# A windowed attention on one NeuronCore: key-side scores recomputed, or query-side weights transposed

## What is computed

```python
q = heads(x @ Wq + bq); k = heads(x @ Wk + bk); v = heads(x @ Wv + bv)
# key index runs over s-128 .. s+128, clipped to the sequence
scores = einsum('bhsd,bhswd->bhsw', q, k_win) / sqrt(8)
scores = where(valid, scores, -inf)
attn = softmax(scores, axis=-1)
out = einsum('bhsw,bhswd->bhsd', attn, v_win)
return out.transpose(0, 2, 1, 3).reshape(B, S, E) @ Wo + bo
```

## Time and profile before

| | us |
|---|---|
| median of 3 runs | 3092.83 (3081.48 to 3099.36) |
| the profiled execution: its time | 3103.04 |
| its span in the trace | 3101.3 |
| PE, DVE, ACT, POOL busy | 2707.9, 1738.0, 1476.6, 1833.4 |
| mean granted PE clock over the span | 0.873 |

### The profile page before, as it was taken

One profiled execution on the slowest core, in us unless ns is written; L12 is line 12 of the kernel. 1 busy time (PEld: TensorE's weight loads), 2 busy tenths in 40 slices (PEclk: granted clock), 3 DMA queues, 4 the chain that ended last, 5 costly groups with the idle time before them and its releaser, 6 DMA issues. The chain is left out here.

```text
span 3101.3 us, 91235 instructions
## 1 busy us (share of the span) xinstructions
PE 2707.9 (87%) x37375; PEld 1824.3 (59%) x37375; DVE 1738.0 (56%) x3395; ACT 1476.6 (48%) x2703; POOL 1833.4 (59%) x3112
## 2 busy tenths in 40 slices
PE   4859999965989999989999999999999958999977
PEld 1228888852666666666666666666666635455445
DVE  5832222214767776677767777777777635334324
ACT  3722232212656666566666566656665622233233
POOL 0045666405988888888888887888888711121111
PEclk9967898756999999999999999999999987577668
DMA  1001111102111212122212212121111100000000
GB/s 31 0 22 34 44 38 35 30 17 110 52 42 50 60 52 71 50 57 60 59 48 63 67 52 57 52 78 43 42 49 45 43 11 13 1 1 1 1 12 14
DMA packets 113143, 124.58 MB, mean 40 GB/s; under 512 B 40782, under 2 KB 71262, under 8 KB 111966
## 3 DMA queue, kind: packets, MB, share of 16 engines
q1 hardware_dynamic: 111808, 117.52, 13.8%
q10 hardware_dynamic: 926, 1.27, 0.1%
HBM read 35.89 MB, written 8.91 MB: 14 GB/s over the span
## 5 line engine op out<-in xcount | busy, mean ns | idle before, releaser
L1719 POOL TENSOR_TENSOR l_rot_a<-l_rot_a,l_rot_b 128x512 f32<-128x512 f32 x384 | 483.9, 1275 | 109.8 <-DVE l_rot_b L1579 109.3
L1207 PE MATMUL l_A<-l_wts,l_H 128*128 128x512 f32 x768 | 416.1, 626 | 25.5 <-ACT l_H L1520 21.5
L1573 DVE TENSOR_TENSOR l_rot_a<-l_A,l_tab 128x512 f32<-128x512 f32 x384 | 264.9, 690 | 288.5 <-ACT l_sq L1439 276.2
L1728 POOL TENSOR_TENSOR l_qk<-l_rot_a,l_rn 128x512 f32<-128x512 f32 x384 | 388.7, 1044 | 21.2 <-POOLq L1766 20.9
L1439 ACT ACTIVATE l_sq<-l_A 128x512 f32<-128x512 f32 x384 | 231.0, 601 | 131.9 <-PE l_A L1207 128.3
L1445 ACT ACTIVATE l_pT<-l_T 128x512 f32<-128x512 f32 x192 | 108.8, 595 | 374.0 <-PE l_T L1253 373.7
L1579 DVE TENSOR_TENSOR l_rot_b<-l_A,l_tab 128x512 f32<-128x512 f32 x384 | 261.4, 681 | 0.0
L1583 DVE TENSOR_REDUCE l_ss<-l_sq 128x8 f32<-128x512 f32 x384 | 259.5, 676 | 0.0
L2048 ACT ACTIVATE a_pT<-a_t 128x384 f32<-128x384 f32 (+1 forms) x256 | 111.1, 463 | 261.4 <-PE a_t L1946 261.3
L1308 PE MATMUL l_T<-ident,l_qk 128*128 128x128 f32 x1536 | 210.3, 279 | 19.6 <-POOL l_qk L1728 14.4
L1308 PEld LDWEIGHTS l_T<-ident,l_qk 128*128 128x128 f32 x1536 | 174.9, 142 | 84.1 <-issue 58.0
(11 more groups left out here) (340 smaller groups left out, 5948.0 us busy)
## 6 DMA issues: line engine op xcount, KB each, us to landing
l_vw<-l_vn SPq DMA_DIRECT2D x384, 128.0 KB
l_vw<-l_vn SPq DMA_DIRECT2D x360, 64.0 KB
l_wts<-in_l_wts SPq DMA_DIRECT2D x18, 650.0 KB, 4.9
c_lower_out<-c_amt SPq DMA_DIRECT2D x16, 384.0 KB, 2.5
c_inv<-c_first_in SPq DMA_DIRECT2D x16, 384.0 KB, 3.4
l_tab<-in_l_tables SPq DMA_DIRECT2D x6, 1024.0 KB, 5.1
l_wts<-in_l_wts SPq DMA_DIRECT2D x6, 635.5 KB, 5.3
result<-x SPq DMA_DIRECT2D x4, 256.0 KB, 2.3
```

Of the source, the lines that this page charges most:

```text
L1207: pe.matmul(A[j % 2][:], cols(m), w_of(m)[:, C_QKV + 512 * j:C_QKV + 512 * j + 512], start=True, stop=True).then_inc(pq_done, 1)
L1573: dve.tensor_tensor(rot_a[p][:, j, :].rearrange("p (a d) -> p a d", d=DH), src.rearrange("p (a d) -> p a d", d=DH), table[:, a, t:t + 1, : ...
L1719: pool.tensor_tensor(rot_a[m % 2][:, j, :], rot_a[m % 2][:, j, :], rot_b[:, j, :], ALU.add).then_inc(rot_rdy, 1)
L1728: pool.tensor_tensor(qk[:, j, :].rearrange("p (a d) -> p a d", d=DH), rot_a[p][:, j, :].rearrange("p (a d) -> p a d", d=DH), rn[p][:, 8 * ...
```

## The change

`turned`, `turn_maxima` and `shift` go. The scores are made once, with queries on partitions. ACT reads them from `s_ps` with `negmax` as the bias of the exponential and writes `p` (two tiles of 16 x 384). POOL clears the corners of `p`. PE then transposes the weights: a chunk is one group of heads and one neighbouring tile, four transposes of 128x128 into one bank of `t_ps`, 12 chunks a tile (8 at the ends of a sequence), 176 in all. Of every three chunks ACT copies two to `pT` and DVE one. A bank of `s_ps` is now free when the exponential has read it. Values of tile t are made in step t+1, a group at a time, and the output parts come in step t+2. The core of the diff:

```diff
-        negmax = [sb(f"a_negmax{i}", [P, QUADS, P]) for i in range(2)]
-        pT = [sb(f"a_pT{i}", [P, AH, SPAN]) for i in range(RING)]
+        negmax = [sb(f"a_negmax{i}", [P, AH]) for i in range(2)]
+        p = [sb(f"a_p{i}", [P, AH, SPAN]) for i in range(2)]
+        pT = sb("a_pT", [P, 3, AH, P])
...
-        TURNED, VALUED = 2, 4
-        STEPS = NT + VALUED
+        STEPS = NT + 2
...
+        def chunks(t):
+            lo, hi = near(t)
+            return [(j, a) for j in range(QUADS) for a in range(lo, hi + 1)]
+        def by_vector(c):
+            return c % 3 == 2
...
 # tensor engine, scores(t, h)
-                    pe.wait_ge(mx_rdy, n - GROUP + 1)
+                    pe.wait_ge(p_rdy, n - GROUP + 1)
...
+            def turn_weights(t, i):
+                j, a = chunks(t)[i]
+                c = FIRST_CHUNK[t] + i
+                pe.wait_ge(sel_rdy, QUADS * t + j + 1)
+                if c >= 2:
+                    if by_vector(c - 2):
+                        pe.wait_ge(pt_dve, vector_chunks(c - 1))
+                    else:
+                        pe.wait_ge(pt_act, act_chunks(c - 1))
+                for g in range(GROUP):
+                    mm = pe.transpose(t_ps[c % 2][:, P * g:P * g + P], p[t % 2][:, GROUP * j + g, P * (1 + a):P * (2 + a)], ident[:])
+                mm.then_inc(pt_done, 1)
...
             for s in range(STEPS):
-                if has(s):
-                    for h in range(GROUP):
-                        scores(s, h)
-                if has(s - 1):
-                    turn_maxima(s - 1)
-                if has(s - VALUED):
-                    values(s - VALUED, (0, 1))
-                for h in range(GROUP, AH):
+                for h in range(AH):
                     if has(s):
                         scores(s, h)
-                    if has(s - TURNED):
-                        turned(s - TURNED, h - GROUP)
-                    if h == 7 and has(s - VALUED):
-                        values(s - VALUED, (2, 3))
-                    if h == 11 and has(s - VALUED):
-                        turn_out(s - VALUED)
...
+                    if has(s - 1) and h < len(chunks(s - 1)):
+                        turn_weights(s - 1, h)
+                    if h == 1 and has(s - 2):
+                        turn_out(s - 2)
+                    if h == 4 and has(s - 2):
+                        turn_heads(s - 2)
+                    if h == 7 and has(s - 2):
+                        project_out(s - 2)
+                    if h >= AH - QUADS and has(s - 1):
+                        values(s - 1, h - (AH - QUADS))
...
 # scalar engine
-                act.wait_ge(t_done, AH * t + h + 1)
-                act.activation(pT[t % RING][:, h, c0:c1], t_ps[h % 2][:, c0:c1], ACT.Exp).then_inc(p_rdy, 1)
+                act.wait_ge(mx_rdy, n + 1)
+                act.activation(p[t % 2][:, h, c0:c1], s_ps[h % GROUP][:, c0:c1], ACT.Exp, bias=negmax[t % 2][:, h:h + 1]).then_inc(p_rdy, 1)
+            def keep_turned(t, i):
+                act.activation(pT[:, 1 + a, GROUP * j:GROUP * j + GROUP, :].rearrange("k h q -> k (h q)"), t_ps[c % 2][:],
+                               ACT.Copy).then_inc(pt_act, 1)
...
             for s in range(STEPS):
+                if has(s - 2):
+                    keep_out(s - 2)
                 for h in range(AH):
-                    if has(s - TURNED):
-                        weights(s - TURNED, h)
+                    if has(s):
+                        weights(s, h)
+                    if has(s - 1) and h < len(chunks(s - 1)) and not by_vector(FIRST_CHUNK[s - 1] + h):
+                        keep_turned(s - 1, h)
+                    if h == 5 and has(s - 2):
+                        keep_heads(s - 2)
...
 # vector engine
-            def shift(t):
-                dve.tensor_tensor(q, m_ps[:].rearrange("p (j q) -> p j q", j=QUADS), q, ALU.add).then_inc(qa_rdy, 1)
+            def keep_turned(t, i):
+                dve.tensor_copy(pT[:, 1 + a, GROUP * j:GROUP * j + GROUP, :].rearrange("k h q -> k (h q)"), t_ps[c % 2][:])\
+                   .then_inc(pt_dve, 1)
```

More of the change, by code:

```diff
@@ L1919, in around, with act_chunks, vector_chunks @@
             return slice(P * (t + lo), P * (t + hi + 1))
+        def chunks(t):
+            lo, hi = near(t)
+            return [(j, a) for j in range(QUADS) for a in range(lo, hi + 1)]
+        FIRST_CHUNK = [sum(len(chunks(i)) for i in range(t)) for t in range(NT + 1)]
+        def by_vector(c):
+            return c % 3 == 2
+        def act_chunks(c):
+            return c - c // 3
+        def vector_chunks(c):
+            return c // 3
         @block.sync
@@ L1958, in values @@
+            def values(t, j):
                 lo, hi = near(t)
-                if quads[0] == 0:
-                    pe.wait_ge(sel_rdy, QUADS * (t + hi) + QUADS)
+                last_chunk = FIRST_CHUNK[t] + (j + 1) * (hi - lo + 1)
+                pe.wait_ge(pt_act, act_chunks(last_chunk))
+                pe.wait_ge(pt_dve, vector_chunks(last_chunk))
+                if j == 0:
                     pe.wait_ge(x_rdy, t)
[L1962 to L1969, removed]
+                for a in range(lo, hi + 1):
+                    for g in range(GROUP):
+                        h = GROUP * j + g
+                        mm = pe.matmul(o_ps[VW * g:VW * g + VW, P * j:P * j + P], v[:, t + a, VS * h:VS * h + VW],
+                                       pT[:, 1 + a, h, :], start=(a == lo), stop=(a == hi), skip_group_check=True)
@@ L2005, in _ @@
             pe.wait_ge(v_rdy, NC)
[L2006 removed]
+            pe.wait_ge(init, 1)
             for s in range(STEPS):
[L2009 to L2016 removed]
+                for h in range(AH):
                     if has(s):
                         scores(s, h)
[L2019 to L2031 removed]
+                    if has(s - 1) and h < len(chunks(s - 1)):
[8 more added lines that the diff above has]
+                        values(s - 1, h - (AH - QUADS))
         @block.scalar
@@ L2117, in _ @@
             dve.wait_ge(bo_rdy, 1)
[L2118 to L2126, removed]
+            for s in range(STEPS):
+                for h in range(AH):
                     if has(s):
                         maxima(s, h)
-                    if h == 11 and has(s - VALUED):
-                        divide(s - VALUED)
+                    if has(s - 1) and h < len(chunks(s - 1)) and by_vector(FIRST_CHUNK[s - 1] + h):
+                        keep_turned(s - 1, h)
+                    if h == 3 and has(s - 2):
+                        divide(s - 2)
+                    if h == 8 and has(s - 2):
+                        add(s - 2)
             dve.wait_ge(x_rdy, NT)
@@ L2143, in clear @@
                 if lo == -1:
-                    part = pT[t % RING][:, heads, 0:P]
+                    part = p[t % 2][:, heads, 0:P]
                     last = pool.affine_select(out=part, in_=part, pattern=[[0, GROUP], [1, P]], compare_op=ALU.is_ge, fill=0.0,
@@ L2147, in clear @@
                 if hi == 1:
-                    part = pT[t % RING][:, heads, 2 * P:3 * P]
+                    part = p[t % 2][:, heads, 2 * P:3 * P]
                     last = pool.affine_select(out=part, in_=part, pattern=[[0, GROUP], [-1, P]], compare_op=ALU.is_ge, fill=0.0,
```

52 lines of the change are left out of this document (21 added, 31 removed).

## The result

| | before | after |
|---|---|---|
| median, us (4 runs each) | 3096.1 (3081.5 to 3102.1) | 3324.86 (3307.7 to 3332.4) |
| loop of the attention in the profile, us | 414.1 | 645.0 |
| mean granted clock in it | 0.67 | 0.51 |
| PE busy in it, us | 378.1 | 637.8 |

The changed kernel takes 1.0739 times the time of before, 95% interval 1.0682 to 1.0796: 228.8 us more by the medians, where 235 were forecast. The time of 3324.86 is 3 us from the 3328 of the prediction.

What follows compares the result with a forecast made beforehand. PE was taken as the bound: scores, chunks, values and outputs at the lower clock sum to 668.6 us, adjusted to a 649 us loop, 235 over 414.1, giving 3338, or 3328 on the median's level; range 3180 to 3370.

Steps and rivals of the forecast that it cites:

- The bound: Attention loop: PE bounds it, busy 378.1 of 414.1 us before the change; PE busy over 95% expected after.
- added waits: PE's chunk waiting for the copy of the chunk two before, longer-held `s_ps` banks, values waiting for copies: costed at zero.
- lone score: One score standing alone between two changes of shape on PE: 1.58 us at 384 columns, lower clock; the least certain step.
- values of a group: Value matmuls of one head group of a tile on PE, six groups of four: 1.43 us at the lower clock.
- a chunk with `turn_out`: A chunk followed by `turn_out` in the same shape on PE: 1.9 us, the longest full-height run left.
- the 41 us that I kept open downwards: 256 scores on PE: some 0.16 us less each if no weight load lay between their two passes.
- no run over 1.9 us is left: PE's new order: full-height runs too short to lift the clock, so it stays at 0.50 until the last tile.
- second rival: Attention loop: clock goes to 1.00 and stays from step 1's first chunks; loop 358 us, kernel 3037; chance 0.10.
- two sums, 649 and 358: Forecast attention loop in us: 649 wholly at the lower clock, 358 at the upper, against 414 before.
- Do transposes count for the clock?: PE's clock: the normalisation's 16 transposes seemed to lift it; the skill says transpose-mode work doesn't engage the full level.
- third rival: PE starts transposes in the array's free quarters, so lone scores cost less; result near no change; chance 0.05.
- ACT and DVE: Per tile ACT 13.5 us and DVE 12.6, covered by PE's 22 or more; exponential's bias up to 0.1 each, taken as nothing.

Runs made afterwards that it cites:

- groups: The changed kernel's instructions reordered on PE: four scores, then that group's chunks, all values of a tile at the step's end; 2964.5 us, 0.9587 times before.
- pairs: The changed kernel with scores and chunks in twos on PE: two scores, then two chunks; 2989.8 us, 0.9671 times before.
- Lifting the clock: The changed kernel with 32 needless transposes added at the head of steps 2 and 10; two executions, 3204.55 and 3067.54 us.
- its repetition: The changed kernel with 32 needless transposes at the head of steps 2 and 10, measured again; six executions: 3086, 3111, 3134, 3188, 3191, 3201 us.

## Why the prediction was right

- **The bound.** Right. PE is busy for 99% of the loop, and the added waits cost it 0.3 us before a chunk and 4.4 before a score (2.2 of them at 384 columns).
- **The prices at the lower clock.** Forecast and measured: a lone score 1.58 and 1.58 (2800.24 to 2801.82), a chunk 1.04 and 1.04 (2801.82 to 2802.86), the values of a group 1.43 and 1.43 (2828.66 to 2830.09), a chunk with `turn_out` 1.90 and 1.90 (2798.34 to 2800.24). So the 41 us that I kept open downwards, for a lone score cheaper than that, were not needed; no run parts its weight load from its passes. The loop came out at 645.0 against 649. The forecast had priced all of it at the lower level, and in the 3.2 us from 2931.8 and in the last 9 us it was at the upper; the 2.4 us that PE was busy in the first of these would be 4.8 at the lower, so I estimate that the two make up most of the 4 us.
- **The clock.** The level was right: 0.51 in the loop's mean, and 0.829 to 0.836 over the span in all four executions, so it is no chance of one. The reason given for it is only half right, and that part was luck. I had written that in the kernel before the clock rose only after 3.76 us of full-height work. The same trace has rises after less. Two more stretches of the kernel before:

```profile
2703.50:2706.40 2.90, 2.27 (x13) 0.86 (x8) 2.06 (x7) 1.30 (x3) 0.00 (x0) 1.00 0.00 0
2812.80:2815.60 2.80, 2.80 (x17) 1.36 (x20) 1.37 (x6) 0.00 (x0) 0.57 (x1) 0.50 0.00 0
2815.90:2829.00 13.10, 11.75 (x150) 7.49 (x139) 8.04 (x31) 4.80 (x14) 1.27 (x2) 1.00 0.01 2
```

```profile
2814.43 1.11 PE L1954 MATMUL a_m<-ident,a_negmax 128*128 128x128 f32 x4
2815.48 1.64 PE L1967 MATMUL a_o<-a_pT,a_v 128*32 128x128 f32 x48
```

  At 2703 it rose behind 2.72 of values alone, between 2815.6 and 2815.9 within 1.5 us of the end of the scores, and near 2867 even among scores and turned scores. So "no run over 1.9 us is left" was no sound ground for "it will not rise", and the changed kernel did rise at 2931. What the runs do show is the direction: with longer runs of full-height work the clock rose and stayed (groups), mostly stayed (pairs), or rose while added transposes ran, and the order decides over the level with the same instructions. The rule behind it stays open, and holding the level is partly chance, as the executions with two additions show. My second rival (the clock goes up and stays) was a real state of this order, its pair priced rightly (1.43 against 1.42); in the traces it held only with added work. By the prediction's two sums, 649 and 358, the clock is the larger part of what the grouped order gains back (645 to 286): about 290 us by this estimate, and some 70 the grouping.
- **Do transposes count for the clock?** I said so from the earlier trace rows, against the Trainium skill ("TensorE: Matmul & The Clock Gate", Part 4: PE-mode transpose). The grouped order, in which transposes are a large share of PE's work, ran at 1.00 from 2640 on, and under "Lifting the clock" and in its repetition the clock rose each of four times while the 32 transposes of the identity ran. The measurements decide, and they differ from the page. That transposes count as much as values is not shown: in the pairs, 2.75 of transposes twice lifted nothing and 2.62 of values twice did.
- **The third rival** (no emptying between shapes) is out: at the lower level 179 lone scores of 384 columns hold PE for 1.57 or 1.58 each.
- **ACT and DVE.** Right to cost at nothing; the exponential's bias took 0.09 of the up to 0.1 that I allowed. It can matter only once the order is mended: 16 x 0.09 = 1.4 us of ACT in a step of the grouped kernel, an estimate that no run tests.
- **The median.** The move of 235 stood on the loop of one execution of before; between the two loops in the traces it was 231, and by medians 229. That the median came within 3 us of 3328 is closer than this working can claim, with 30 us of spread ahead of the loop.

## What to carry to other kernels

Count array time by shape, not by columns: on PE four 32-row matmuls next to each other cost what one costs alone between two changes of shape, so interleaving kinds of matmul instruction by instruction undoes the sharing. When such a loop runs at the lower clock, try the order first, with the same instructions grouped by shape and full-height work in long runs: here it turned 7% slower into 4% faster, without one matmul more. And when a change halves a kind of work but splits it finely, work out the loop at both clock levels before believing either.

## What was not expected of the hardware

- One kernel, the changed order with two additions, ran at either level of the clock within one execution (156 us at the upper, 297 at the lower), and its eight executions lie between 3068 and 3205 us. At each level it keeps an exact pace, 1.42 or 2.62 us a pair.
- Work that nothing needs made the kernel 206 us faster (3324.86 to 3118.7).
- A per-partition bias from SBUF costs an exponential of 384 columns 0.09 us (0.491 to 0.580). The Trainium skill ("ScalarE: Activation LUTs", What ACT_TABLE_LOAD costs) gives about 93 ns for each per-partition operand; the run agrees (89 ns).
